# Three-layer graph kernel on one core: six pairs of gathered rows instead of four in the two attention walks, and the chain of segment maxima handed over in other pieces

## The chip, the cores and the metric

One core of one Trainium2 chip runs the whole program. The metric is the device time of one execution in microseconds (us), lower is better.

## The reference, cut to what matters

The program computes a graph-attention layer, a mixture of experts, a second graph layer and a routed feed-forward layer, all added to x. Only the attention layer is touched. It runs twice, first with 2 heads of 128 and then with 1 head of 256, over the same 100000 edges (sorted by destination) among 6250 nodes:

```python
z = (x @ W).reshape(num_nodes, heads, d)
el = jnp.einsum('nhd,hd->nh', z, a_l)
er = jnp.einsum('nhd,hd->nh', z, a_r)
e = el[src] + er[dst]
e = jnp.where(e > 0, e, NEG_SLOPE * e)
m = jax.ops.segment_max(e, dst, num_segments=num_nodes)
ex = jnp.exp(e - m[dst])
s = jax.ops.segment_sum(ex, dst, num_segments=num_nodes)
alpha = ex / s[dst]
msg = z[src] * alpha[:, :, None]
out = jax.ops.segment_sum(msg, dst, num_segments=num_nodes)
```

The second graph layer is a weighted mean over the same edges: it gathers in the same way and has no segment maxima.

## The kernel before

The phases follow one another: plan, rows1, walk1, walk2, post, dispatch, experts, combine, walk3, route, ffn. Walk1 and walk2 are `edge_walk` with two heads and with one head, walk3 is the weighted mean (another function, which the diff does not touch). In walk1 the node work of the layer between the two attentions rides along (`node`: a load of finished sums, a transpose, a product with the next weights, a store).

**Edges.** The sorted edges make 98 groups of 1024, each of 8 tiles of 128 edges (one edge per partition). One group is one step, two steps are one pair, so a walk has 98 steps, 49 pairs. The sums of a step go into a window of 80 nodes (`WIN`).

**What each engine does for a step or a pair.**

- GpSimd (POOL) gathers: `gather(s, k)` waits until the step that used the buffer before is done (`done8`) and until its indices stand in `idx[k]` (`idx_ready`), then issues 8 indirect DMAs (L583), one for each tile, 128 rows of z each. The rows go to `Z[k // 2]`; z carries el as an extra column.
- SyncE (SP) loads three small things for each pair (er of the window, two tables of resets): `load`, three pairs ahead (`AHEAD`).
- VectorE (DVE) finds the segment maxima of el (the chain, below), builds the one-hot tiles (`hot`, L803), looks up er for each edge (`targets`, L810 and L812), forms the logits (`logits`), scales (`hots`, L870 in walk1), and in walk1 divides the node sums (`node.scale`).
- ScalarE (ACT) takes the exponentials (`exps`, L610), scales rows or one-hot tiles by them (`scale`, 16 instructions per pair), and in `window` waits for the products of a step (`done8`), copies the next indices into `idx[k]` (`copy_idx`, L596), copies the window's sums out of PSUM (L633) and stores them.
- TensorE (PE) multiplies one-hot tiles by rows (`products`, L730, 8 matmuls per step in four quarters), and turns small things for the chain.

**The chain of maxima.** The maximum of e over a segment is taken from the maximum of el. For pair p: PE transposes the el column of the 16 tiles (`turn_el`, L693); DVE scans each tile from both sides (`scan_el`, L817 and L818; increments `ends_ready`); PE transposes the two end columns into one row (`turn_ends`, L699 and L700; `ends_turned`); DVE scans over the tiles (`carries`, L828 and L830, each head on its own; `ins_ready`); PE turns the carries back into columns (`turn_ins`, L705 and L706; `ins_turned`); DVE copies them (L837) and scans again with them (`scan_maxima`, L839 and L841; `max_ready`); PE transposes the result (`columns`, L711 and L712; `cols`); DVE forms the logits from it. That is three hand-overs DVE to PE and four PE to DVE for a pair, all in order. While PE multiplies pair p, both engines do the chain of pair p+2: `turn_el` behind quarter 0 of the first step, `turn_ends` behind quarter 2, `turn_ins` behind quarter 0 of the second step, `columns` at the end of the pair.

**Buffers.** `UNROLL = 8` steps are written out per turn of the loops, with one buffer each for indices and local targets and one `Z` for each two steps: four pairs of rows lie on chip, and the gathers of pair p+4 can start when pair p is done. Walk3 has eight step buffers too.

## Time and profile before

| | |
|---|---|
| three timed runs | 5286.85, 5288.94, 5299.87 us, median 5288.94 |
| profiled execution | 5308.62 us (span 5306.6), mean granted TensorE clock 0.749 |
| PE busy | 3058.9 us, 58% of the span |
| POOL busy | 2681.1 us, 51% |
| DVE busy | 1986.9 us, 37% |
| ACT busy | 1502.5 us, 28% |
| walk1 | from its first gather at 215 us to the end of its node work at 1571 us |
| walk2 | 1571 to 2805 us |
| walk3 | 3620 to 4870 us |

The span is that of one profiled execution, 19.7 us above the median of the timed runs. The busy shares are means over all phases: no engine is near 100%, and within a walk each engine waits for another one. What counts is therefore which wait ends last in each pair of steps.

### The profile page before, as it was taken

The page shows a single profiled execution, that of the slowest core. Times are in us where ns is not written, and L with a number is a line of the kernel's source. Part 1 is how long each engine was busy: PE and PEld are TensorE (multiplying, and loading weights), DVE is VectorE, ACT ScalarE, POOL GpSimd, SP SyncE. Part 2 cuts the span into 40 slices and gives each one's busy share as a digit, 9 for nine tenths or more (in the row PEclk, how much of TensorE's full clock was granted, in tenths as well). Part 3 has the DMA queues.
Part 4 walks back from the last instruction along what each step waited for, and adds up shares of the span by engine and source line. Part 5 has one row for each costly group of instructions (what it writes and reads, how often), then busy time and mean ns, then how long its engine had stood idle before and what let it go on. Part 6 is the DMA issues. An engine that isn't in the chain of part 4 may idle for free. (4 is left out here: it accounts for less than half of the span.)

```text
span 5306.6 us, 61698 instructions
## 1 busy us (share of the span) xinstructions
PE 3058.9 (58%) x11768; PEld 1883.0 (35%) x11768; DVE 1986.9 (37%) x5614; ACT 1502.5 (28%) x4807; POOL 2681.1 (51%) x2732
## 2 busy tenths in 40 slices
PE   3245555555543455554554489921566666666699
PEld 2123333332321222222223478820333333333466
DVE  4246555555533333333336812242222222223222
ACT  2122232332221222222221023311334444444233
POOL 1366666666626666666652145525566666661121
PEclk9667767777766767677775699965777777777799
DMA  6346666666623433333334266675444444442111
GB/s 151 82 97 104 107 106 109 107 108 104 104 52 96 98 95 99 97 97 98 95 90 135 64 200 220 225 226 153 108 123 120 122 119 122 120 122 65 63 55 51
DMA packets 381422, 598.24 MB, mean 113 GB/s; under 512 B 102442, under 2 KB 272078, under 8 KB 380658
## 3 DMA queue, kind: packets, MB, share of 16 engines
q0 software_dynamic: 136000, 386.29, 32.0%
q1 hardware_dynamic: 209138, 172.22, 12.0%
q10 hardware_dynamic: 36160, 38.56, 2.4%
q14 instruction: 104, 0.85, 0.1%
q8 instruction: 20, 0.33, 0.0%
HBM read 489.46 MB, written 107.34 MB: 112 GB/s over the span
## 5 line engine op out<-in xcount | busy, mean ns | idle before, releaser
L583 POOL DMA_INDIRECT walk_rows<-z_two_heads,walk_idx x784 | 794.7, 1014 | 536.3 <-ACT walk_idx L596 302.5
L583 POOL DMA_INDIRECT walk_rows<-z_one_head,walk_idx x784 | 758.3, 967 | 534.6 <-ACT walk_idx L596 301.9
L1861 POOL DMA_INDIRECT walk_rows<-h,walk_idx x784 | 747.5, 953 | 460.6 <-issue 232.8
L2006 PE MATMUL walk_ps_part<-walk_rows,walk_whot 128*80 128x257 f32 x1568 | 538.3, 479 | 244.1 <-issue 138.2
L730 PE MATMUL walk_ps_part<-walk_rows,walk_hot 128*80 128x258 f32 x1568 | 527.4, 469 | 0.6
L730 PE MATMUL walk_ps_part<-walk_rows,walk_whot 128*80 128x257 f32 x1568 | 519.0, 478 | 0.0
L2006 PEld LDWEIGHTS walk_ps_part<-walk_rows,walk_whot 128*80 128x80 f32 x1568 | 266.5, 186 | 441.4 <-issue 405.9
L596 ACT ACTIVATE walk_idx<-keep_src 128x8 int32 x212 | 44.1, 208 | 1293.5 <-remote 952.1
L730 PEld LDWEIGHTS walk_ps_part<-walk_rows,walk_whot 128*80 128x80 f32 x1568 | 267.9, 186 | 175.9 <-issue 127.1
L730 PEld LDWEIGHTS walk_ps_part<-walk_rows,walk_hot 128*80 128x80 f32 x1568 | 254.7, 180 | 132.2 <-issue 72.8
L812 DVE TENSOR_REDUCE walk_er<-walk_picked 128x8 f32<-128x640 f32 x294 | 241.0, 820 | 29.4 <-issue 7.6
L810 DVE TENSOR_TENSOR walk_picked<-walk_hot,walk_erB 128x640 f32<-128x640 f32 x294 | 241.0, 820 | 22.0 <-issue 3.1
L705 PE MATMUL walk_ps_row_scores<-walk_ones,walk_ends 1*32 1x1 f32 (+1 forms) x196 | 20.4, 171 | 384.2 <-DVEq L832 219.2
L624 ACT ACTIVATE walk_rows<-walk_rows,walk_w 128x129 f32<-128x129 f32 x784 | 235.3, 389 | 5.8
L699 PE MATMUL walk_ps_row_scores<-keep_ident,walk_fmax 32*1 32x32 f32 (+1 forms) x98 | 18.5, 188 | 369.6 <-issue 239.2
L1585 PE MATMUL exp_ps_hid<-exp_hT,exp_w 128*128 128x256 f32 x864 | 220.2, 388 | 8.3 <-DMA exp_b<-in_ffn_b 5.7
L1577 PE MATMUL exp_ps_y<-exp_w,exp_g 128*128 128x256 f32 x864 | 222.6, 380 | 0.0
L2120 DVE TENSOR_TENSOR walk_n_y<-walk_n_h,walk_ps_n_rows 128x256 f32<-128x256 f32 x52 | 21.9, 421 | 522.1 <-DMA walk_n_agg<-agg 459.0
L621 ACT ACTIVATE walk_whot<-walk_hot,walk_w 128x80 f32<-128x80 f32 x784 | 202.9, 347 | 20.5 <-issue 12.8
L1887 ACT ACTIVATE walk_whot<-walk_hot,walk_weight 128x80 f32<-128x80 f32 x784 | 206.8, 349 | 0.0
L828 DVE TENSOR_TENSOR_SCAN walk_ends<-walk_rr,walk_ends,walk_ps_row_scores 1x16 f32<-1x16 f32 x147 | 32.9, 224 | 453.1 <-remote 387.4
L1529 POOL DMA_INDIRECT y_tokens<-exp_y,exp_home x108 | 106.1, 982 | 183.1 <-DVE exp_y L1617 166.6
(368 smaller groups left out, 5189.3 us busy)
## 6 DMA issues: line engine op xcount, KB each, us to landing
exp_w<-in_ffn_W SPq DMA_DIRECT2D x108, 512.0 KB
agg<-walk_window ACTq DMA_DIRECT2D x198, 80.3 KB
walk_rows<-z_two_heads,walk_idx POOLq DMA_INDIRECT x784
walk_rows<-z_one_head,walk_idx POOLq DMA_INDIRECT x784
comb_ya<-y_tokens POOLq DMA_DIRECT2D x28, 448.0 KB
walk_rows<-h,walk_idx POOLq DMA_INDIRECT x784
walk_erB<-er_two_heads SPq DMA_DIRECT2D x104, 80.0 KB
agg<-walk_window ACTq DMA_DIRECT2D x99, 80.6 KB
```

What stands on the lines that cost most here:

```text
L583: pool.indirect_dma_start(out=Z[k // 2][:, k % 2 * GROUP_TILES + t, :], out_offset=None, in_=table, in_offset=bass.IndirectOffsetOnAxis(ap ...
L621: last = act.activation(S[k % HOTS][:, t, :], S0[k % HOTS][:, t, :], ACT.Copy, scale=w[:, 0, col:col + 1])
L624: last = act.activation(row, row, ACT.Copy, scale=w[:, 1, col:col + 1])
L730: last = pe.matmul(P[k % 2][0:WIN, 0:AW].rearrange("p (h w) -> p h w", w=HW), hot[:, t, :], rows, start=t == 0, stop=t == GROUP_TILES - 1)
L810: dve.tensor_tensor(picked[:, :, :], S0[k % HOTS][:, :, :], erB[q][:, j, :, h].unsqueeze(1).to_broadcast(wide), ALU.mult)
L812: dve.tensor_reduce(er[:, h, j * GROUP_TILES:(j + 1) * GROUP_TILES], picked[:, :, :], axis=AX.X, op=ALU.add)
L1529: pool.indirect_dma_start(out=dram["ys"], out_offset=bass.IndirectOffsetOnAxis(ap=home[k][:, t:t + 1], axis=0), in_=y[k][:, t, :], in_offs ...
L1577: last = pe.matmul(psY[k][t][:, 0:D], g[k][:, hc, t * 128:(t + 1) * 128], W2[k][:, hc, :], start=hc == 0, stop=hc == HC - 1)
L1585: last = pe.matmul(psH[hc % 2][:, 0:BLOCK], W1[k][:, hf, hc * 128:(hc + 1) * 128], hT[k][:, hf, :], start=hf == 0, stop=hf == HALVES - 1)
L1861: pool.indirect_dma_start(out=Z[k // 2][:, k % 2 * GROUP_TILES + t, :], out_offset=None, in_=table, in_offset=bass.IndirectOffsetOnAxis(ap ...
L1887: last = act.activation(S[k % HOTS][:, t, :], S0[k % HOTS][:, t, :], ACT.Copy, scale=weight[k][:, t:t + 1])
L2006: last = pe.matmul(P[k % 2][0:WIN, 0:HW], S[k % HOTS][:, t, :], Z[k // 2][:, k % 2 * GROUP_TILES + t, :], start=t == 0, stop=t == GROUP_TI ...
```

## The change

It changes `edge_walk` only (walk1 and walk2), the tables of `plan` that it reads, and nothing of walk3. Its parts:

1. **Depth.** In `edge_walk`, 12 steps are written out per turn in place of 8: six `Z` buffers in place of four, twelve `idx` and `dloc`, six of each of the small inputs, and 8 turns of the loop in place of 12. `AHEAD` goes from 3 to 5, `LOCAL_AHEAD` from 6 to 8. The plan computes the turns of these loops separately (five more small DVE instructions, two more numbers in a table).
2. **One hand-over of each kind for a pair.** `ends_ready`, `ends_turned`, `ins_ready` and `ins_turned` go; `el_scanned`, `rows_turned` and `rows_ready` come. PE's `turn_rows(r)` turns the end columns of pair r and the carries of pair r-1 together, with one increment of `rows_turned`; DVE's `scan_rows(r)` answers with the carries of pair r (`rows_ready`) and the maxima of pair r-1 (`max_ready`). A pair now has three hand-overs from DVE to PE and three from PE to DVE.
3. **Order.** While PE multiplies pair p it does `columns(p+1)` first, `turn_rows(p+3)` between the two steps, and `turn_el(p+4)` at the end. DVE does `weights(p+1)`, `scores(p+2)` (now only one-hot tiles and er, without a wait for PE), `node.scale(p+1)`, `scan_rows(p+3)`, `scan_el(p+4)`.
4. **Copies.** Since the transposed el must outlive its PSUM tile, `scan_el` copies it to `el_rows` (32x128 with two heads, 16x128 with one); `firsts` takes the place of `foremost` and the first of `ends`, with one more small copy; the el transpose has a PSUM bank of its own.
5. **Start.** Before its first product PE turns el of pairs 0 to 3, so it waits for the gathers of four pairs there; before, for those of two.

```diff
+EDGE_UNROLL = 12
+EDGE_LOOPS = (GROUPS - 2) // EDGE_UNROLL
...
-STEP_TAB = 2 * 96
+STEP_TAB = 2 * 104
...
+            dve.tensor_scalar(nie[:, :], ends[0:1, GROUPS - 1:GROUPS], float(GROUPS) + 0.5,
+                              float(EDGE_LONG - EDGE_LOOPS), ALU.is_gt, ALU.mult)
...
+    UNROLL = EDGE_UNROLL
...
-        LOCAL_AHEAD = 6
+        LOCAL_AHEAD = 8
...
-        AHEAD = 3
+        AHEAD = 5
...
-            def turn_ends(p):
-                pe.wait_ge(ends_ready, p + 1)
...
-            def turn_ins(p):
-                pe.wait_ge(ins_ready, p + 1)
...
+            def turn_rows(r, ends_too, ins_too):
+
+                if ends_too:
+                    pe.wait_ge(el_scanned, r + 1)
+                    pe.sem_inc(row_tick, 1)
+                if ins_too:
+                    pe.wait_ge(rows_ready, r)
+                    pe.sem_inc(row_tick, 1)
+                    pe.matmul(psK[:, 0:1], ends[:, 0:PT, :].rearrange("o t h -> o (t h)"), ones[:, 0:1], start=True, stop=True)
+                    last = pe.matmul(psK[:, 1:2], begins[:, 1:CT1, :].rearrange("o t h -> o (t h)"), ones[:, 0:1],
+                                     start=True, stop=True)
+                if ends_too:
+                    pe.transpose(psR[:, 0:ROWS], Fl[:, TILE - 1:TILE], ident[0:ROWS, 0:ROWS])
+                    last = pe.transpose(psR[:, ROWS:2 * ROWS], Bl[:, 0:1], ident[0:ROWS, 0:ROWS])
+                last.then_inc(rows_turned, 1)
...
+            def pair(p, m, s, turn, on):
+
+                if on(1):
+                    columns(p + 1, (m + 1) % 2)
                 products(s, 2 * m, 0)
-                if turn is not None:
-                    turn_el(p + 2, b, turn)
                 products(s, 2 * m, 1)
                 if node:
                     node.turn(pe, p, m % 2)
                 products(s, 2 * m, 2)
-                if turn is not None:
-                    turn_ends(p + 2)
                 products(s, 2 * m, 3)
                 if node:
                     node.products(pe, p, m % 2)
...
+                if on(2):
+                    turn_rows(p + 3, on(3), True)
+                for quarter in range(4):
                     products(s + 1, 2 * m + 1, quarter)
-                if turn is not None:
-                    columns(p + 2)
+                if on(4):
+                    turn_el(p + 4, (m + 4) % PAIRS, turn)
...
             for p in range(2):
                 turn_el(p, p, 1)
-                turn_ends(p)
-                turn_ins(p)
-                columns(p)
+                turn_rows(p, True, p > 0)
+            turn_el(2, 2, 1)
+            columns(0, 0)
+            turn_rows(2, True, True)
+            turn_el(3, 3, 1)
...
+            def scan_el(p, q, k, loaded):
+                dve.wait_ge(inputs[q], loaded)
                 dve.wait_ge(el_turned, p + 1)
...
+                dve.tensor_copy(el_rows[k][:, :], psT[:, :])
+                dve.drain().then_inc(el_scanned, 1)
+
+            def scan_rows(r, q, k, ends_too, ins_too):
+
+                dve.wait_ge(rows_turned, r + 1)
+                if ins_too:
+                    dve.tensor_copy(gkc[:, :], psK[:, :])
+                if ends_too:
...
+                    dve.tensor_copy(ends[:, 0, :], ends[:, PT, :])
+                    dve.drain()
...
+                    dve.drain()
+                    dve.tensor_tensor(firsts[k][:, 0, :], ends[:, 0, :], begins[:, 0, :], ALU.max)
+                    dve.tensor_copy(firsts[k][:, 1, :], ends[:, 0, :])
+                dve.drain().then_inc(rows_ready, 1)
...
                 weights(p + 1, m + 1, s + 2)
-                if turn is not None:
-                    scores(p + 2, m + 2, s + 4, turn)
+                if on(2):
+                    scores(m + 2, s + 4)
                 if node:
                     node.scale(dve, p + 1, (m + 1) % 2, half)
+                if on(2):
+                    scan_rows(p + 3, (m + 3) % INS, (m + 3) % 2, on(3), True)
+                if on(4):
+                    scan_el(p + 4, (m + 4) % INS, m % 2, loaded)
```

## Rows read from the trace of the kernel before

**Rows 1.** Windows of walk1, walk2, walk3: busy us (instructions) by engine, granted clock, DMA.

```profile
215.00:1571.00 1356.00, 727.75 (x2762) 404.61 (x2762) 732.79 (x1779) 380.00 (x1397) 794.67 (x784) 0.71 0.58 100
1571.00:2805.00 1234.00, 609.90 (x2254) 315.25 (x2254) 401.20 (x1133) 291.12 (x1141) 758.31 (x784) 0.71 0.38 95
3620.00:4870.00 1250.00, 767.95 (x2636) 429.82 (x2636) 290.16 (x965) 502.02 (x1623) 747.51 (x784) 0.74 0.43 115
```

**Rows 2.** Page, costliest groups: the gathers of the three walks.

```profile
L583 POOL DMA_INDIRECT walk_rows<-z_two_heads,walk_idx x784 | 794.7, 1014 | 536.3 <-ACT walk_idx L596 302.5
L583 POOL DMA_INDIRECT walk_rows<-z_one_head,walk_idx x784 | 758.3, 967 | 534.6 <-ACT walk_idx L596 301.9
L1861 POOL DMA_INDIRECT walk_rows<-h,walk_idx x784 | 747.5, 953 | 460.6 <-issue 232.8
```

**Rows 3.** Waits of POOL, 300:1478, 1667:2742, 3761:4783: us, times, longest.

```profile
POOL walk_rows L583 <- ACT walk_idx L596: 232.6, 54, 16.0
...
POOL walk_rows L583 <- ACT walk_idx L596: 198.0, 48, 11.7
...
POOL walk_rows L1861 <- ACT walk_idx L1874: 176.7, 43, 4.8
```

**Rows 4.** Source lines of the window copies: ns min/median/max, first and last start.

```profile
L633 ACT ACTIVATE walk_window<-walk_ps_part x90: 362/364/383, 313.0 to 1461.1; 80x258 f32<-80x258 f32 x90
L633 ACT ACTIVATE walk_window<-walk_ps_part x7: 363/364/382, 1477.8 to 1526.8; 80x258 f32<-80x258 f32 x7
...
L633 ACT ACTIVATE walk_window<-walk_ps_part x89: 362/364/383, 1666.6 to 2742.1; 80x257 f32<-80x257 f32 x89
```

**Rows 5.** Timeline of POOL: end of the first burst and restart, walk1 and walk2.

```profile
215.08 1.04 POOL L583 DMA_INDIRECT walk_rows<-z_two_heads,walk_idx  x1 [69.64 <-ACT walk_idx L596]
...
297.03 0.95 POOL L583 DMA_INDIRECT walk_rows<-z_two_heads,walk_idx  x1 [0.30 <-issue]
313.93 1.15 POOL L583 DMA_INDIRECT walk_rows<-z_two_heads,walk_idx  x1 [15.95 <-ACT walk_idx L596]
...
1667.51 0.97 POOL L583 DMA_INDIRECT walk_rows<-z_one_head,walk_idx  x1 [11.66 <-ACT walk_idx L596]
```

**Rows 6.** Timeline of POOL, PE, DVE and ACT around one burst of walk2.

```profile
2085.85 0.95 POOL L583 DMA_INDIRECT walk_rows<-z_one_head,walk_idx  x1 [4.50 <-ACT walk_idx L596]
...
2104.71 0.95 POOL L583 DMA_INDIRECT walk_rows<-z_one_head,walk_idx  x1 [0.30 <-issue]
...
2093.69 1.53 PE L730 MATMUL walk_ps_part<-walk_rows,walk_whot 128*80 128x257 f32 x6
2105.08 0.19 PE L705 MATMUL walk_ps_row_scores<-walk_ones,walk_ends 1*16 1x1 f32 x2 [9.87 <-issue]
...
2108.98 0.21 ACT L596 ACTIVATE walk_idx<-keep_src 128x8 int32 x1 [14.51 <-remote]
...
2104.59 0.23 DVE L828 TENSOR_TENSOR_SCAN walk_ends<-walk_rr,walk_ends,walk_ps_row_scores 1x16 f32<-1x16 f32 x1 [11.19 <-remote]
```

**Rows 7.** Waits of all engines in walk1, 400 to 1400 us.

```profile
DVE walk_gkc L837 <- remote: 209.3, 15, 17.1
...
PEld walk_ps_cols L711 <- DVEq L843: 186.2, 17, 14.0
```

**Rows 8.** Timeline of ACT, window copies at the end of walk2 (seven).

```profile
2774.38 0.36 ACT L633 ACTIVATE walk_window<-walk_ps_part 80x257 f32<-80x257 f32 x1
...
2801.77 0.36 ACT L633 ACTIVATE walk_window<-walk_ps_part 80x257 f32<-80x257 f32 x1
```

**Rows 9.** Timeline of PE in the first burst of walk3.

```profile
3688.88 1.02 PE L2005 MATMUL walk_ps_part<-walk_window,walk_carry 80*1 80x257 f32 x2 [36.36 <-issue]
```

**Rows 10.** Groups by line, DVE in walk1, 500 to 1400 us.

```profile
L817 DVE TENSOR_TENSOR_SCAN walk_fmax<-walk_reset,walk_ps_row_scores 32x128 f32<-32x128 f32 x35 | 14.1, 402 | 10.9 <-remote 9.3 <-issue 1.6
...
L837 DVE COPY walk_gkc<-walk_ps_row_scores 32x2 f32<-32x2 f32 x35 | 5.2, 147 | 212.9 <-remote 181.5 <-issue 26.2 <-PE walk_ps_row_scores L706 4.3
```

**Rows 11.** Source line L583 in walk1: ns min/median/max, first and last start.

```profile
L583 POOL DMA_INDIRECT walk_rows<-z_two_heads,walk_idx x784: 947/953/1630, 215.1 to 1475.4; - x196
```

More of the change, by code:

```diff
@@ L479, in edge_walk @@
         M = ph.sb("smax", [ROWS, TILE])
-        row_ends = ph.sb("ends", [1, 1 + CT1, H])
-        foremost, ends = row_ends[:, 0, :], row_ends[:, 1:CT1 + 1, :]
+        ends = ph.sb("ends", [1, CT1, H])
+        firsts = [ph.sb(f"firsts{k}", [1, 2, H]) for k in range(2)]
+        el_rows = [ph.sb(f"el_rows{k}", [ROWS, TILE]) for k in range(2)]
         begins = ph.sb("begins", [1, CT1, H])
@@ L532, in load @@
             def load(p, q):
[L533 removed]
+                sp.wait_ge(inputs_used6, p + 1)
                 sp.sem_inc(sp_tick, 1)
@@ L819, in scan_el @@
                                        ALU.add, ALU.max)
-                dve.tensor_copy(ends[:, 0, :], ends[:, PT, :])
-                dve.drain().then_inc(ends_ready, 1)
-            def carries(p, q):
-                dve.wait_ge(ends_turned, p + 1)
-                turned = psR[:, :].rearrange("o (c t h) -> o c h t", c=2, h=H)
-                reset = rr[q][:, :, :, :, :].rearrange("o c h j t -> o c h (j t)")
-                for h in range(H):
-                    dve.tensor_tensor_scan(ends[:, 1:CT1, h], reset[:, 0, h, :], turned[:, 0, h, :],
-                                           ends[:, 0, h:h + 1], ALU.add, ALU.max)
-                    dve.tensor_tensor_scan(begins[:, PT - 1::-1, h], reset[:, 1, h, ::-1], turned[:, 1, h, ::-1],
-                                           -BIG, ALU.add, ALU.max)
-                dve.drain().then_inc(ins_ready, 1)
-                dve.tensor_tensor(foremost, ends[:, 0, :], begins[:, 0, :], ALU.max)
@@ new lines, in scan_el @@
+                dve.drain().then_inc(el_scanned, 1)
[4 more added lines that the diff above has]
+                if ends_too:
+                    turned = psR[:, :].rearrange("o (c t h) -> o c h t", c=2, h=H)
+                    reset = rr[q][:, :, :, :, :].rearrange("o c h j t -> o c h (j t)")
+                    dve.tensor_copy(ends[:, 0, :], ends[:, PT, :])
+                    dve.drain()
+                    for h in range(H):
+                        dve.tensor_tensor_scan(ends[:, 1:CT1, h], reset[:, 0, h, :], turned[:, 0, h, :],
+                                               ends[:, 0, h:h + 1], ALU.add, ALU.max)
+                        dve.tensor_tensor_scan(begins[:, PT - 1::-1, h], reset[:, 1, h, ::-1], turned[:, 1, h, ::-1],
+                                               -BIG, ALU.add, ALU.max)
+                    dve.drain()
+                    dve.tensor_tensor(firsts[k][:, 0, :], ends[:, 0, :], begins[:, 0, :], ALU.max)
+                    dve.tensor_copy(firsts[k][:, 1, :], ends[:, 0, :])
+                dve.drain().then_inc(rows_ready, 1)
+                if ins_too:
+                    before = (q + INS - 1) % INS
+                    dve.tensor_tensor_scan(Cf, R[before][:, 0:TILE], el_rows[1 - k][:, :], gkc[:, 0:1], ALU.add, ALU.max)
+                    dve.drain()
+                    dve.tensor_tensor_scan(M[:, TILE - 1::-1], R[before][:, TILE:0:-1], Cf[:, TILE - 1::-1], gkc[:, 1:2],
+                                           ALU.add, ALU.max)
+                    dve.drain().then_inc(max_ready, 1)
@@ L871, in hots, with scores @@
                 last.then_inc(hot_ready, 1)
-            def scores(p, m, s, loaded):
-                q = m % INS
-                dve.wait_ge(inputs[q], loaded)
-                scan_el(p, q)
+            def scores(m, s):
                 hot(s, 2 * m % UNROLL)
                 hot(s + 1, (2 * m + 1) % UNROLL)
-                carries(p, q)
-                targets(q, 0, 2 * m % UNROLL)
-                scan_maxima(p, q)
-                targets(q, 1, (2 * m + 1) % UNROLL)
+                dve.drain()
+                for j in range(2):
+                    targets(m % INS, j, (2 * m + j) % UNROLL)
             def weights(p, m, s):
@@ L890, in weights, with pair @@
                 hots(s + 1, (2 * m + 1) % UNROLL, W[m % 2])
-            def pair(p, m, s, half, turn):
+            def pair(p, m, s, half, loaded, on):
                 weights(p + 1, m + 1, s + 2)
-                if turn is not None:
-                    scores(p + 2, m + 2, s + 4, turn)
+                if on(2):
+                    scores(m + 2, s + 4)
                 if node:
                     node.scale(dve, p + 1, (m + 1) % 2, half)
+                if on(2):
+                    scan_rows(p + 3, (m + 3) % INS, (m + 3) % 2, on(3), True)
+                if on(4):
+                    scan_el(p + 4, (m + 4) % INS, m % 2, loaded)
             n, rest = turns(dve), rest_of(dve)
-            scores(0, 0, 0, LOADS)
+            for p in range(2):
+                scan_el(p, p, p % 2, LOADS)
+                scan_rows(p, p, p % 2, True, p > 0)
+            scan_el(2, 2, 0, LOADS)
+            scores(0, 0)
             weights(0, 0, 0)
-            scores(1, 1, 2, LOADS)
+            scan_rows(2, 2, 0, True, True)
+            scores(1, 2)
+            scan_el(3, 3, 1, LOADS)
             if node:
```

73 lines of the change are left out of this document (27 added, 46 removed).

## The prediction, made before the changed kernel ran

> **What bounds the kernel now.** I read the windows by stage first. In none of the three walks is an engine full: POOL, the busiest, has 795, 758 and 748 us of 1356, 1234 and 1250, and the DMA engines are at 0.58, 0.38 and 0.43 [rows 1]. Then the costliest groups: the gathers are the same 784 in each walk, and what releases them after idle time is the ACT copy of the next indices [rows 2]. That copy waits for the products of the step that held the buffer, so POOL waits for the consumers.
>
> A gather takes 1014, 967 or 953 ns [rows 2] and 0.30 us of issue follows it [rows 5], so the 16 of a pair cost 16 x 1.314 = 21.0 us in walk1, 16 x 1.267 = 20.3 in walk2, 16 x 1.253 = 20.0 in walk3. The waits for a released buffer, without the first one, are (232.6 - 16.0)/45 = 4.8 us per pair in walk1, (198.0 - 11.7)/44 = 4.2 in walk2, and 176.7/43 = 4.1 each in walk3 [rows 3]. The sums are 25.8, 24.5 and 24.1 us per pair. The window copies give the same: 313.0 to 1477.8 us for 90 steps is 25.9 per pair, 1666.6 to 2742.1 for 88 steps is 24.4 [rows 4].
>
> The reader is to see two things. First, walk3, which has no chain of maxima at all, is only 0.3 us per pair faster than walk2. Second, the shape of a period in the timeline: 16 gathers start from 2085.85 to 2104.71. PE finished a step at about 2095.2 (1.53 us of L730 from 2093.69), yet ACT saw it at 2108.98; DVE went on with L828 at 2104.59 after 11.19 us, and PE with L705 at 2105.08 after 9.87 [rows 6]. So hand-overs made in the second half of a burst of gathers are seen about when it ends, and POOL's gap of 4 us is what lies between the burst's end and the release that was late. The first burst of walk3 shows the same without any chain: PE idle for 36.36 us in it [rows 9]. I call this the hold. I don't know its cause, only its shape.
>
> Walk1's extra against walk2 is 25.9 - 24.4 = 1.5 us per pair. Half of it is the gather itself (0.7), the rest gaps: 53 waits for 45 pairs, where walk2 has 47 for 44 [rows 3]. Here the chain shows: PE's weight load at `columns` waits 186.2 us for DVE's L843 in 1000 us, DVE 209.3 us at L837 [rows 7].
>
> **The change, part by part.**
>
> *Start.* 96 gathers fit before POOL waits, where 64 did. 32 more at 1.256 us (0.95 + 0.30 [rows 5]) are 40.2 us. In walk1 the first release came 313.0 - 215.1 = 97.9 us after the first gather [rows 4, 5], 80.4 of it the burst; PE now waits for four pairs there and is held besides. I put all 40.2 us on the path, in each walk. The lower bound is 0, if step 0 were done within the burst; walk3's first is, but that burst held PE for 36 us [rows 9].
>
> *End.* After the last gather six pairs are on chip in place of four. Without gathers a pair takes (1526.8 - 1477.8)/3.5 = 14.0 us in walk1 (eight copies, of which the profile holds seven [rows 4]) and (2801.77 - 2774.38)/3 = 9.1 in walk2 [rows 8]. So two pairs of the steady part move to this pace: 43 steady pairs stay in walk1 (of 45) and 42 in walk2 (of 44).
>
> *Hand-overs.* One of four from PE to DVE goes, and the three left stand a pair or two ahead of their use; `turn_el(p)` waits for rows released two pairs before, no longer one. A late hand-over delays the chain only if it is more than about half a pair late. Bounds of walk1's period: below, that of walk3, 24.1, above, today's 25.9. If every extra gap goes and the slower gathers stay, it is 21.0 + 4.2 = 25.2; if the slower gathers go too, 24.4. I take the middle, 24.8. In walk2 the bounds are 24.1 and 24.4, and I take 24.3.
>
> *DVE's added work.* The copy of el to `el_rows` is at most a scan of the same tile (402 ns, L817) and at least L837's 147 ns; the second copy to `firsts` is one like L837 [rows 10], and there are two drains more. Together 0.3 to 0.9 us per pair. DVE is busy 733 of 1356 us in walk1, 15.0 us per pair [rows 1], so its cover is the 25.9 - 15.0 = 10.9 us per pair in which it waits. Without it, it would cost 0.9 x 49 = 44 us in walk1. I take nothing.
>
> *Moved:* `turn_rows`, `columns` and `turn_el` issue the same six kinds of small PE matmuls as before. No DMA and no queue of POOL or SP is moved; SP's loads run five pairs ahead in place of three, 6 small loads more at the start, under the 120 us burst. Behind DVE's new wait at `scan_rows` stand `scan_el(p+4)` and `weights(p+2)`, for which ACT's exponentials and then PE's next products wait; it hangs on PE's half pair. *Plan:* five small DVE instructions and a drain, at 0.15 to 0.2 us, about 1 us, uncovered. *Loops:* 8 turns for 12, nothing.
>
> *A rule against it.* Walk1's gathers have a median of 953 ns but reach 1630 [rows 11], a mean of 1014 [rows 2], so something lengthens some of them. The Trainium skill ("SBUF — State Buffer", "A bandwidth-pool intuition that's wrong") says that an fp32 copy from SBUF to SBUF on DVE locks GpSimd out of writing its descriptors, so that DMAs from its queue starve. The trace agrees in kind only: it does not show which DVE instruction stood beside a long gather. By that rule the added SBUF copy would lengthen gathers, and the time would be rival E's below; by the rows alone, which price the copy at 147 ns beside idle time, it adds nothing.
>
> **The sum**, against the profiled execution of 5308.6 us:
> Walk1: 40.2 + 43 x 24.8 + 2 x 14.0 - 1164.8 = -30.2.
> Walk2: 40.2 + 42 x 24.3 + 2 x 9.1 - 1075.5 = +3.5.
> Plan: +1. Together -25.7, so 5282.9 us profiled. The profiled execution stood 19.7 us above the median of the runs shown; the forecast as a median is 5263 us.
>
> **The rivals.**
>
> *B, longer bursts pay.* With six pairs on chip and a looser chain the consumers may release two pairs between waits, and the gap of 4.2 us comes once in two pairs: 21.0 + 2.1 = 23.1 in walk1, 20.3 + 2.1 = 22.4 in walk2. For it: walk2's first 64 gathers with their gap of 11.66 us [rows 5] come to (64 x 1.267 + 11.4)/64 = 1.44 us per gather, 23.1 per pair. Against it: the consumers stand still in a long burst and have to catch up after it, and POOL restarts at the first released step, however many buffers there are. Sum: walk1 -103, walk2 -76, so 5110 us. At its far end POOL never waits (21.0 and 20.3 per pair): -194 and -165, so 4931 us.
>
> *D, only the gaps go.* Walk1 at 25.2, walk2 at 24.4 as before: 68.2 + 43 x 25.2 - 1164.8 = -13, walk2 58.4 + 42 x 24.4 - 1075.5 = +8, plan +1: 5285 us, no change.
>
> *C, the other side: the longer first burst is paid and the pace stays.* If the hold and not the chain sets walk1's 25.9, the fewer hand-overs are hidden anyway and both walks lose their start: 68.2 + 43 x 25.9 - 1164.8 = +17, walk2 +8, plan +1: 5315 us; and if the consumers catch up slowly, so that the end gives nothing back, up to 5289 + 2 x 40.2 = 5369. For it: walk2 and walk3 have the same period with and without a chain. Against it: walk1's waits at L711 and L837, which walk3 has not. It decides from a walk1 period of about 25.8 on.
>
> *E, longer gathers.* If the added work lengthens one gather of each pair from 953 to 1630 ns [rows 11], that is 0.68 x 98 = 66 us on the forecast: 5329. Against it: walk1's DVE does nearly twice walk2's work [rows 1] and its gathers are only 47 ns longer in the mean [rows 2]. The Trainium skill's rule above is what would make this one.
>
> **How the numbers follow.** 0.3% (16 us) is what a measurement of this kernel can tell from no change. Chances: my forecast 0.40, B 0.14 and its far end 0.03, D 0.21, C 0.19, E 0.03. The forecast's own range goes from 24.4 to 25.1 us per pair in walk1 and reaches half the start's cost up, 5240 to 5295; 0.06 of its 0.40 lies within 0.3% of no change. So faster is 0.34 + 0.17 = 0.51, same 0.21 + 0.06 = 0.27, slower 0.19 + 0.03 = 0.22. The range takes in B, E and most of C: 5105 to 5335; outside are B's far end, C's upper part and some of B, under 0.2 together.
>
> **What the profile after would show.** The first wait of POOL in each walk after 96 gathers, some 40 us later than now. In between, waits of about 4 us, 45 or fewer per walk; B would show half as many. The waits at `columns` behind the second scan's drain and at the copy of the carries should all but vanish in walk1 if the chain mattered; walk3 should not move. Gathers should keep their means of 1014 and 967 ns; longer ones would speak for the skill's rule. The forecast is wrong if the gaps stay at 4.8 us per pair in walk1 (C), or if POOL's wait falls below 3 us per pair (B).

## The result, and the profile after

The changed kernel takes 5351.1 us (median of 4 runs, 5348.1 to 5389.5), the kernel before 5290.5 (5286.9 to 5299.9): a ratio of 1.0117, 95% interval 1.0089 to 1.0145. It is slower by some 60 us, where 26 us of gain were forecast. The profiled execution of after has a span of 5346.4 us, 39.8 above that of before. The profile of before stood 18 us above its median and that of after 3 us below its own, so 21 of the 60 us stand in no stretch of the two profiles.

Page of after, costliest groups: the gathers, to be held against [rows 2].

```profile
L595 POOL DMA_INDIRECT walk_rows<-z_two_heads,walk_idx x784 | 808.3, 1031 | 502.0 <-ACT walk_idx L608 264.0
L595 POOL DMA_INDIRECT walk_rows<-z_one_head,walk_idx x784 | 771.8, 984 | 550.2 <-ACT walk_idx L608 322.3
L1885 POOL DMA_INDIRECT walk_rows<-h,walk_idx x784 | 749.4, 956 | 468.7 <-issue 235.8
```

Source lines of the window copies in after (ns min/median/max, first and last start): the first 85 steps of walk1, its last 13, the first 85 of walk2, and its last 14, of which the first is the 85th again.

```profile
L645 ACT ACTIVATE walk_window<-walk_ps_part x85: 363/365/383, 356.3 to 1428.1; 80x258 f32<-80x258 f32 x85
...
L645 ACT ACTIVATE walk_window<-walk_ps_part x13: 363/370/383, 1440.9 to 1552.3; 80x258 f32<-80x258 f32 x13
...
L645 ACT ACTIVATE walk_window<-walk_ps_part x85: 361/365/384, 1723.1 to 2752.8; 80x257 f32<-80x257 f32 x85
...
L645 ACT ACTIVATE walk_window<-walk_ps_part x14: 363/364/372, 2752.8 to 2829.3; 80x257 f32<-80x257 f32 x14
```

The same lines of before, for the same steps:

```profile
L633 ACT ACTIVATE walk_window<-walk_ps_part x85: 362/364/383, 313.0 to 1401.7; 80x258 f32<-80x258 f32 x85
...
L633 ACT ACTIVATE walk_window<-walk_ps_part x14: 362/364/382, 1401.7 to 1530.2; 80x258 f32<-80x258 f32 x14
...
L633 ACT ACTIVATE walk_window<-walk_ps_part x85: 362/364/383, 1666.6 to 2697.5; 80x257 f32<-80x257 f32 x85
```

Timeline of POOL in after: first gather of walk1, the restart after 96 gathers.

```profile
220.57 1.03 POOL L595 DMA_INDIRECT walk_rows<-z_two_heads,walk_idx  x1 [79.06 <-ACT walk_idx L608]
...
343.27 0.95 POOL L595 DMA_INDIRECT walk_rows<-z_two_heads,walk_idx  x1 [0.30 <-issue]
357.18 1.41 POOL L595 DMA_INDIRECT walk_rows<-z_two_heads,walk_idx  x1 [12.96 <-ACT walk_idx L608]
```

The reader can take the 39.8 us of the two spans apart with these:

| stretch | before | after | difference |
|---|---|---|---|
| first gather of walk1 | 215.1 | 220.6 | +5.5 |
| walk1: first gather to first window copy | 97.9 | 135.7 | +37.8 |
| walk1: 42 pairs (84 steps) | 1088.7, 25.92 per pair | 1071.8, 25.52 per pair | -16.9 |
| walk1: from there to the last copy | 128.5 | 124.2 | -4.3 |
| to the first gather of walk2 | 44.6 | 40.2 | -4.4 |
| walk2: first gather to first window copy | 91.8 | 130.6 | +38.8 |
| walk2: 42 pairs | 1030.9, 24.55 per pair | 1029.7, 24.52 per pair | -1.2 |
| walk2: from there to the last copy | 104.3 | 76.5 | -27.8 |
| all behind it (walk3 +10.0, unchanged code) | 2504.8 | 2517.1 | +12.3 |

So the first window copy comes as much later as was forecast, in both walks. What was to pay for it, walk1's pace, is little better, and walk1 gives nearly nothing back at its end.

The prediction said that the two waits of [rows 7] would all but vanish in walk1 if the chain mattered. One did. In walk1 of after, from 400 to 1400 us, DVE at the copy of the carries, and PE's weight load at `columns`:

```profile
DVE walk_gkc L840 <- remote: 3.2, 1, 3.2
...
PEld walk_ps_cols L726 <- issue: 107.8, 25, 9.9
PEld walk_ps_cols L726 <- DVEq L861: 55.0, 14, 12.5
```

DVE's was 209.3 us and is gone. PE's at `columns` is 163 us in two rows, 108 of it without a releaser that the profile shows, where it was 194 (186.2, and 8.2 without one). And PE now waits at the product of the node work too, for the Relu of ACT that makes its input. Before and after, in the same window:

```profile
PEld walk_ps_n_z L411 <- ACT walk_n_hT L385: 25.1, 6, 6.6
```

```profile
PEld walk_ps_n_z L421 <- ACT walk_n_hT L395: 166.9, 21, 15.1
```

### The profile page after: what moved, and what is told of

Same layout as the page of the kernel before. It is cut to its first block and busy times, and to the rows that moved or that the text cites. A ratio compares the mean times of both kernels' runs of the same rounds, so it can differ in the third digit from the quotient of the medians.

```text
span 5346.4 us, 62209 instructions
## 1 busy us (share of the span) xinstructions
PE 3052.7 (57%) x11768; PEld 1912.8 (36%) x11768; DVE 2027.2 (38%) x5813; ACT 1508.1 (28%) x4819; POOL 2711.4 (51%) x2732
## 5 line engine op out<-in xcount | busy, mean ns | idle before, releaser
L595 POOL DMA_INDIRECT walk_rows<-z_two_heads,walk_idx x784 | 808.3, 1031 | 502.0 <-ACT walk_idx L608 264.0
L595 POOL DMA_INDIRECT walk_rows<-z_one_head,walk_idx x784 | 771.8, 984 | 550.2 <-ACT walk_idx L608 322.3
L2030 PE MATMUL walk_ps_part<-walk_rows,walk_whot 128*80 128x257 f32 x1568 | 530.7, 474 | 219.3 <-issue 125.7
L745 PE MATMUL walk_ps_part<-walk_rows,walk_hot 128*80 128x258 f32 x1568 | 513.9, 479 | 3.4 <-issue 3.4
L745 PE MATMUL walk_ps_part<-walk_rows,walk_whot 128*80 128x257 f32 x1568 | 505.6, 478 | 4.8 <-issue 4.8
L742 PE MATMUL walk_ps_part<-walk_window,walk_carry 80*1 80x129 f32 (+1 forms) x588 | 137.1, 345 | 491.6 <-ACT walk_window L645 478.6
L745 PEld LDWEIGHTS walk_ps_part<-walk_rows,walk_hot 128*80 128x80 f32 x1568 | 276.8, 189 | 157.1 <-issue 105.9
L421 PE MATMUL walk_ps_n_z<-walk_n_w,walk_n_hT 128*128 128x258 f32 x208 | 98.7, 623 | 311.6 <-ACT walk_n_hT L395 174.9
L742 PEld LDWEIGHTS walk_ps_part<-walk_window,walk_carry 80*1 80x1 f32 x588 | 33.6, 82 | 576.8 <-ACT walk_window L645 503.9
```

Source lines behind the costliest of these rows:

```text
L595: pool.indirect_dma_start(out=Z[k // 2][:, k % 2 * GROUP_TILES + t, :], out_offset=None, in_=table, in_offset=bass.IndirectOffsetOnAxis(ap ...
L742: pe.matmul(P[k % 2][0:1, cols], CE[k % HOTS][:, h:h + 1], wsb[1 - k % 2][:, cols], start=False, stop=False)
L745: last = pe.matmul(P[k % 2][0:WIN, 0:AW].rearrange("p (h w) -> p h w", w=HW), hot[:, t, :], rows, start=t == 0, stop=t == GROUP_TILES - 1)
L2030: last = pe.matmul(P[k % 2][0:WIN, 0:HW], S[k % HOTS][:, t, :], Z[k // 2][:, k % 2 * GROUP_TILES + t, :], start=t == 0, stop=t == GROUP_TI ...
```

## Two regimes

The first experiments went to another chip, and it showed something that no profile before had: POOL never waited for long for a released buffer. Every walk was one burst of 784 gathers, and the same kernel before took 4667 us in place of 5290. I had not expected this. The waits of POOL in the kernel before there (run e12, from 230 to 1300 us), against [rows 3]:

```profile
POOL walk_rows L583 <- issue: 222.5, 730, 0.3
POOL walk_rows L583 <- ACT walk_idx L596: 9.4, 31, 0.3
```

and its gathers and last window copies of walk1, beside those of the changed kernel on the same chip (run e13):

```profile
L583 POOL DMA_INDIRECT walk_rows<-z_two_heads,walk_idx x784: 949/953/1602, 216.5 to 1284.2; - x196
...
L633 ACT ACTIVATE walk_window<-walk_ps_part x7: 363/364/383, 1284.6 to 1332.7; 80x258 f32<-80x258 f32 x7
```

```profile
L595 POOL DMA_INDIRECT walk_rows<-z_two_heads,walk_idx x784: 949/953/1597, 231.9 to 1295.7; - x196
...
L645 ACT ACTIVATE walk_window<-walk_ps_part x9: 363/371/383, 1298.4 to 1363.0; 80x258 f32<-80x258 f32 x9
```

I call the regime of the first profiles the waiting one (the first measurement, e5 to e7, e16 to e18) and this one the free one (e1 to e4, e8 to e15). Each of the groups e1 to e4, e5 to e7, e8 to e11, e12 to e15 and e16 to e18 ran on one chip, the first and the third group on the same one, and each ratio is against the kernel before on that chip in that group. In the free regime the hand-overs are not held up in a burst (the first window copy of e12 comes 72 us after its first gather, while POOL gathers on for 1068 us; in before it came after 98 us, behind the burst of 64), a gather costs what it cost in the waiting one (953 ns in the median), and the gathers alone set the pace: 1.36 us each in walk1, 20.5 us per pair in walk2. What makes a chip show the one or the other stays open. The granted clock in walk1 is 0.71 in before and 0.74 in e12, so nearly the same.

## The experiments

**e1, depth alone.** The old chain, with twelve steps written out:

```diff
+    UNROLL = EDGE_UNROLL
...
-        AHEAD = 3
+        AHEAD = 5
```

(with the tables of the plan).

> The chain of maxima as before, but twelve steps and six pairs of rows on chip, loads five pairs ahead, and the plan's table as in the change. Theory S (the first burst of gathers is paid and the pace stays with the hold): both walks start some 40 us later than before and their pace is 25.9 and 24.5 us per pair as before; about +10 us in walk2, +17 to +25 in walk1, so the whole kernel is as slow as the changed one, 5340 to 5360 us. Rival K (the new chain costs what the depth would have gained): without the new chain depth shows its worth, walk1 below 25 us per pair and the kernel at or under 5290 us. Rival P (the plan and its table cost several us): the first gather of walk1 comes at 220 us, not 215.

Free regime: 4685.5 us against 4666.7, 1.0041 (1.0028 to 1.0055). The sign of rival P is there, a first gather at 225.5 us, but its cause is not: e8 and e9 below put it down to the loads of SP, and with the weights first the first gather of the changed kernel, with the longer plan, comes no later than that of the kernel before (180.4 and 182.0 us). Neither S nor K was tested.

**e2, depth alone, held to four pairs.**

```diff
-                pool.wait_ge(done8, s + 1)
+                pool.wait_ge(done8, s + 5)
```

> As the run with depth alone, but POOL waits for four steps more before each gather, so that only four pairs are ever on chip: what is left of the change is the loops' form, the loads further ahead and the plan's table. Theory S: the time of the kernel before, 5285 to 5300 us, plus at most the few us of a later first gather; the first gap comes after 64 gathers. Rival L (the longer loop bodies or the plan cost the time): as slow as the changed kernel, 5340 us or more.

1.0041 (1.0026 to 1.0057), the same as e1. In the free regime depth is worth nothing and costs nothing; its surroundings cost some 20 us, 13 of them ahead of the first gather (229.3 us, against 216.5 in e12, the kernel before on another free chip). Neither expectation was tested.

**e3, the changed kernel held to five pairs** (`s + 3` in that wait).

> The changed kernel, but POOL waits for two steps more before each gather: five pairs on chip, the first burst 80 gathers. Theory S: each walk's first release comes 20 us earlier than in the changed kernel, the pace stays within 0.3 us per pair, and walk2's end takes one pair less at the fast pace (-20 + 15): in all 10 to 25 us faster than the changed kernel, 5325 to 5340 us. Rival K2 (the new chain needs the depth): turn_el waits for rows, walk1 and walk2 go to 26 us per pair or more, and the kernel is slower than the changed one.

1.0105 (1.0081 to 1.0129); free regime, where POOL had nothing to wait for, so it told nothing of the first burst (e17 does).

**e4, the first burst split.**

```diff
...
+            for j in range(UNROLL):
+                gather(j + 2, (j + 2) % UNROLL, max(j + 3, UNROLL + 1 if j + 2 >= 8 else 0))
...
-            with pool.Fori(0, n) as i:
+            with pool.Fori(0, rest_of(pool)) as i:
...
```

> The changed kernel, but in the first turn the gathers of steps 8 to 11 wait until step 0 is done, so that the first burst is 64 gathers and the depth is filled up later. Theory S1 (the consumers stand still for as long as POOL gathers, so 32 gathers more cost 40 us wherever they stand): the first window copy comes 38 us earlier, but the burst behind it is 32 gathers or more longer, and from step 20 on all is as in the changed kernel: 5340 to 5360 us. Rival S2 (only the first release counts): the walks keep the 38 us and the kernel comes to 5280 us or less.

1.0153 (1.0129 to 1.0176). In the free regime the two pauses of 13 and 11 us that it adds to a POOL that never waits are simply paid: against e3, which never waits there either, 4740.4 - 4717.8 = 22.6 us. Neither theory was tested.

**e5, the kernel before.**

> The kernel before, unchanged, for its profile beside the others of this call. In the four runs so far POOL never waited for a released buffer: all 784 gathers of a walk were one burst of 1.27 to 1.36 us each. Theory F (there are two regimes, and in the free one the gathers alone set a walk's pace): this kernel shows the same, a pace of 20.5 us per pair in walk2, and its first gather of walk1 some 5 us before the 225 to 229 us seen in those. Rival: with the buffers of before, POOL waits here as it did in the first profile, 24.5 us per pair.

Waiting regime, 5310.5 us. The rival held: the same kernel took 4667 us beside e1 to e4, and on each chip all kernels showed one regime, so it goes with the chip, not with the kernel.

**e6, the changed kernel.**

> The changed kernel, unchanged, beside the others of this call. Theory F: where the gathers alone set the pace, more depth changes nothing in it, and the change costs only its start and its end: PE's first product waits for the rows of pair 3 (two pairs later) and every product stays two pairs further behind the gathers, so that at the end of walk1 and walk2 two pairs more are left when the last gather is out. With 16 to 17 us per pair in walk1 and 9 to 13 in walk2 that is about 45 us, and 5 us more from the plan: a ratio of 1.010 to 1.012. Rival (depth helps or hurts beyond that): a pace in walk2 more than 0.3 us per pair off the 20.5 of the kernel before.

1.0101 (1.0063 to 1.0139), the first result again. First gather at 229.6 us, 12.7 later than e5. The chip was a waiting one, so theory F was not tested here (e13 does).

**e7, one wait of the new chain in the old one.** To e1 was added:

```diff
+                if late is not None:
+                    rows_landed((m + 4) % PAIRS, late)
```

`rows_landed` waits for the two steps of gathers of pair p+4, at the end of pair p; PE also waits so for pairs 2 and 3 before its first product.

> The old chain with six pairs on chip, and one thing of the new one: at the end of pair p PE also waits until the rows of pair p+4 have landed, and at the start for those of pairs 2 and 3. Nothing else is added. Theory F (the wait for rows two pairs further ahead is the whole cost): this is as slow as the run of the changed kernel, within 10 us, so 20 to 30 us slower than the old chain with six pairs (which was at 1.0041 of the kernel before, this at 1.009 to 1.012). Rival C (the new chain's copies, drains and order cost the time): within 5 us of the old chain's 1.0041.

Waiting regime: 1.0147 (1.0101 to 1.0194). The median is 19.5 us above that of the changed kernel (e6), but the intervals overlap, and they overlap with that of the same kernel without the wait (e16, on another chip) too. So in this regime the run decides nothing on the wait.

**e8 and e9, node weights first**, in the changed kernel and in the kernel before:

```diff
+            if node:
+                node.start_sp(sp)
             for p in range(AHEAD + 1):
                 load(p, p % INS)
             if node:
-                node.start_sp(sp)
                 node.load(sp, 0, 0, row_of(sp, 0), None, None)
```

> The changed kernel, but SP issues walk1's four loads of node weights ahead of the loads of the first pairs, where both kernels have them behind. Theory Q (walk1's first gather waits, by way of ACT's and DVE's start, for the last of those weights, and SP's 12 loads of steps at 3.5 us each stand ahead of them, 8 in the kernel before): the first gather comes at about 187 to 192 us, not at 220 to 230, and the whole kernel is 30 to 40 us faster than the changed one, which puts it at a ratio of 1.002 to 1.005 to the kernel before. Rival: the first gather stays where it was, since something else holds it.

> The kernel before with the same one edit: node weights ahead of the loads of the first pairs. Theory Q: the first gather at 187 to 192 us where it was at 215 to 217, and the kernel 22 to 28 us faster than before, a ratio of 0.995 to 0.996. Rival: the gain is lost, because the loads of the first pairs now come later and the first scans wait for them; then within 5 us of the kernel before.

Free regime: the changed kernel goes to 1.0012 (1.0002 to 1.0021), from 1.0116 (e13), the kernel before to 0.992 (0.9904 to 0.9937). Between the two, with this edit in both, 39 us remain (4675.1 - 4636.1). Both gain more than expected. First gathers at 180.4 and 182.0 us. SP's queue in after (first load of a step, last weight), then in e9:

```profile
172.22 0.39 SPq L550 DMA_DIRECT2D walk_erB<-er_two_heads  x1
...
215.58 0.43 SPq L362 DMA_DIRECT2D walk_n_bcol<-in_b_gat  x1
```

```profile
175.18 0.41 SPq L349 DMA_DIRECT2D walk_n_w<-in_W  x1
...
176.62 0.43 SPq L352 DMA_DIRECT2D walk_n_bcol<-in_b_gat  x1
178.63 0.35 SPq L538 DMA_DIRECT2D walk_erB<-er_two_heads  x1
```

In after the weights stand 43 us behind the first load, and ACT's first index copy waits for them:

```profile
219.42 0.21 ACT L608 ACTIVATE walk_idx<-keep_src 128x8 int32 x1 [59.49 <-DMA walk_n_bcol<-in_b_gat]
```

**e10, e11: e1 and e3 again.**

> Once more the old chain with six pairs on chip; it has been run only on a chip where POOL never waited. If POOL waits here for released buffers as in the first profiles: theory S says that the first release of each walk comes 38 to 44 us later than before and walk1's pace is 25.6 to 25.9 us per pair as before, while the new chain has 25.2 to 25.5; the kernel at a ratio of 1.010 to 1.013. The rival, that depth alone brings the pace down, has walk1 at 25.3 or below. If POOL never waits here: 1.004 as before.

> Once more the changed kernel held to five pairs on chip. If POOL waits for released buffers here: theory S says that both walks release first 20 us earlier than the changed kernel, keep its pace within 0.3 us per pair, and give 9 to 16 us less back at the end of each; 10 to 20 us faster than the changed kernel, a ratio of 1.006 to 1.009. Rival K2 (the new chain needs all six): a pace above 26 in walk1 or 25 in walk2, and slower than the changed kernel. If POOL never waits here: 1.0105 as before.

Free regime both: 1.0042 (1.0027 to 1.0056) and 1.0096 (1.0079 to 1.0113), as the first time.

**e12 to e15, four kernels on one chip.**

> The kernel before, unchanged, for a profile on the chip of this call. Where POOL never waits for a released buffer: first gather of walk1 at 215 to 217 us, one burst of 784 gathers in each walk, 20.5 us per pair in walk2, the last gather of walk1 some 45 to 50 us ahead of its last window copy. Where POOL waits: as in the first profile.

> The changed kernel, unchanged, on the chip of this call. Where POOL never waits: theory F, 0 us from the pace, 13 us from SP's longer start, and 30 to 35 us because PE waits for rows two pairs further ahead (later first product, 20 to 25 us more left at the end of walk1 and 11 at the end of walk2): a ratio of 1.009 to 1.012 and no difference to the same kernel held to five pairs. Where POOL waits: 1.010 to 1.012 as before, and 38 to 44 us from the first burst in each walk.

> The old chain with six pairs and PE's wait for the rows of pair p+4 at the end of pair p. It was slower than the changed kernel where POOL waits (1.0147). Where POOL never waits, theory F gives it the changed kernel's time within 10 us: 1.008 to 1.012. Rival C (the new chain's own work costs the time): 1.004 to 1.005, as the old chain with six pairs without that wait.

> The kernel before with the node weights ahead of the loads of the first pairs. Where POOL never waits: a ratio of 0.992 as before, the first gather at 182 us. Where POOL waits: the same 33 us at the start, and nothing given back, since the pace does not hang on it: 5311 - 33, a ratio of 0.994. Rival: where POOL waits, the start is taken back by later waits and the ratio is 0.998 or more.

Free regime. e13, the changed kernel: 1.0116 (1.0099 to 1.0133). e14, the old chain with the one wait: 1.0101 (1.0080 to 1.0123), where it is 1.0041 and 1.0042 without it (e1, e10). So that wait alone costs some 28 us in this regime. The new chain's own work (rival C of this run) is left with at most the 0.0015 between e13 and e14, 7 us, which their intervals don't tell from nothing. e15: 0.9941 (0.9919 to 0.9963).

The spans of e12 and e13 (4669.4 and 4717.7 us) differ by 48.3: first gather 216.5 to 231.9, +15.4; walk1 from first gather to last copy 1116.2 to 1131.1, +14.9, in which the gathers end 3.9 us sooner and the last copy comes 18.8 us later behind them; walk2 1035.5 to 1049.0, +13.5, of which 10.2 behind the last gather; all else +4.5. PE's waits from 350 to 1250 us in e12 and e3 show who is late in this regime, the rows themselves:

```profile
PE walk_ps_row_scores L693 <- DMA walk_rows<-z_two_heads,walk_idx: 363.7, 41, 10.9
```

```profile
PE walk_ps_el L705 <- DMA walk_rows<-z_two_heads,walk_idx: 255.5, 34, 12.1
```

`turn_el` waits there for rows of pair p+4 in place of p+2, before products whose rows landed long ago.

**e16 to e18, the waiting regime.**

> The old chain with six pairs on chip, sent again for a chip on which POOL waits for released buffers. There: theory S, the first burst is 96 gathers and the first release 38 to 44 us later in each walk, walk1's pace 25.6 to 25.9 us per pair (the new chain: 25.2 to 25.5), the ratio 1.008 to 1.012. Rival: depth alone brings walk1 to 25.3 or below and the ratio is 1.006 or less. Where POOL never waits: 1.004 again.

> The changed kernel held to five pairs on chip, sent again for a chip on which POOL waits. There: theory S, first release in each walk 20 us earlier than in the changed kernel, 10 to 17 us less given back at the end, pace as in the changed kernel: a ratio of 1.007 to 1.010 against its 1.010 to 1.012. Rival K2: turn_el comes to wait for rows, pace above 26 us in walk1, ratio above 1.012. Where POOL never waits: 1.010 again.

> The kernel before with the node weights ahead of the loads of the first pairs, sent again for a chip on which POOL waits. There: first gather at 182 to 187 us, 30 us ahead of before, and the kernel 30 us faster, a ratio of 0.993 to 0.996; the rival, that later waits take it back, has 0.998 or more. Where POOL never waits: 0.992 to 0.994 again.

e16, depth alone: 1.0125 (1.0100 to 1.0151), the start as theory S has it and the kernel a little slower; its rival is out. e17, the new chain on five pairs: 0.9983 (0.9971 to 0.9996), which neither theory had: S wanted 1.007 to 1.010, and it misjudged what the sixth pair costs. e18: 0.9956 (0.9936 to 0.9976), as expected. The window copies of the first 85 steps: e16 walk1 and walk2, e17 walk1 and walk2, e18 walk1.

```profile
L644 ACT ACTIVATE walk_window<-walk_ps_part x85: 362/364/383, 355.8 to 1462.3; 80x258 f32<-80x258 f32 x85
...
L644 ACT ACTIVATE walk_window<-walk_ps_part x85: 362/364/382, 1737.1 to 2787.6; 80x257 f32<-80x257 f32 x85
```

```profile
L645 ACT ACTIVATE walk_window<-walk_ps_part x85: 362/365/383, 347.9 to 1408.5; 80x258 f32<-80x258 f32 x85
...
L645 ACT ACTIVATE walk_window<-walk_ps_part x85: 363/364/383, 1700.4 to 2702.1; 80x257 f32<-80x257 f32 x85
```

```profile
L634 ACT ACTIVATE walk_window<-walk_ps_part x85: 363/365/383, 291.6 to 1367.0; 80x258 f32<-80x258 f32 x85
```

All profiles of the waiting regime: from the first gather to the first and to the 13th window copy, the pace of the 42 pairs behind the first copy and of the 36 behind the 13th, and the whole from first gather to last copy, walk1 / walk2:

| kernel | first copy | 13th copy | pace of 42 | pace of 36 | whole |
|---|---|---|---|---|---|
| old chain, 4 pairs (before; e5; e18) | 98, 98, 107 / 92, 92, 91 | 254, 250, 260 / 240, 240, 239 | 25.9, 25.6, 25.6 / 24.5, 24.3, 24.5 | 25.9, 25.6, 25.6 / 24.5, 24.2, 24.5 | 1315, 1315, 1317 / 1227, 1223, 1225 |
| old chain, 6 pairs (e16) | 126 / 113 | 293 / 282 | 26.3 / 25.0 | 26.1 / 24.5 | 1346 / 1243 |
| the same with the late wait (e7) | 131 / 117 | 291 / 281 | 26.1 / 25.1 | 26.0 / 24.7 | 1337 / 1246 |
| new chain, 6 pairs (after; e6) | 136, 136 / 131, 136 | 284, 286 / 280, 282 | 25.5, 25.2 / 24.5, 24.4 | 25.6, 25.2 / 24.4, 24.4 | 1332, 1312 / 1237, 1236 |
| new chain, 5 pairs (e17) | 120 / 122 | 265 / 260 | 25.3 / 23.9 | 25.4 / 24.0 | 1307 / 1213 |

The two paces differ because the first six pairs belong to the start. In walk2 of e16 ACT copied the first indices at 1736.97 us, inside POOL's burst (1623.9 to 1755.3), and the next ones only at 1772.64, behind it:

```profile
1736.97 0.21 ACT L607 ACTIVATE walk_idx<-keep_src 128x8 int32 x1 [41.79 <-remote]
...
1772.64 0.21 ACT L607 ACTIVATE walk_idx<-keep_src 128x8 int32 x1 [33.64 <-remote]
```

So the first copy is too early a mark for the cost of the burst, and a pace counted from it holds a part of that cost. From the 13th copy to the 85th, walk2 takes the same time with four pairs (e18) and with six (e16):

```profile
L634 ACT ACTIVATE walk_window<-walk_ps_part x73: 363/365/383, 1785.9 to 2668.1; 80x257 f32<-80x257 f32 x73
```

```profile
L644 ACT ACTIVATE walk_window<-walk_ps_part x73: 362/364/382, 1905.6 to 2787.6; 80x257 f32<-80x257 f32 x73
```

## Why the prediction was wrong

The time, 5351, lies above the range (5105 to 5335), and the sign was wrong. What came is nearest to rival C (0.19): the longer first burst is paid and the pace stays, or nearly. With the measured paces, 25.5 and 24.5, the forecast's own sum gives +13 us in place of -26; the two profiles are 39.8 apart, and of the other 27 us 20 are walk1's end and 12 lie behind walk2, with 5 the other way. Step by step:

- *Start, right in the waiting regime.* 40.2 us on the path in each walk were counted. The first copy comes 37.8 and 38.8 us later; at the 13th copy it is 31 and 41 us (before and after), 36 and 41 (e5 and e6). Held to five pairs (e17) the 13th copy comes 21 and 22 us sooner than in e6, for 20 us of gathers. Depth alone does it too: 43 us in walk2 and 33 in walk1 (e16 against e18). In the free regime, where no buffer is waited for, the first copy is 25 and 23 us later all the same (e12 and e13), which is PE's wait for four pairs at the start (the old chain with that wait, e14, has 93 and 91 us to the first copy, without it, e1, 73 and 69).
- *Pace of walk1, the step that failed.* The forecast said: "I take the middle, 24.8." Measured are 25.5 and 25.2, against 25.9 and 25.6: 0.4 us per pair and 17 us in all, where 46 were counted (behind the 13th copy 0.3 and 0.4). The bound of 24.4 took walk1's extra gaps for waits of the chain that would go with it. DVE's wait at the carries did go, and the gaps of POOL nearly stayed: PE's wait at `columns` is 163 us where it was 194, and in front of the node product it waits for ACT 166.9 us where it waited 25.1 (e6: 162 and 168.3; e5: 167 and 14.5). PE's idle time moved more than it shrank. Depth alone (e16) lowered DVE's wait to 109.6 us and PE's at `columns` to 93, at a pace no better than before, so these waits are not what holds POOL. What does set walk1's pace, the node product or the hold, no run here takes apart. POOL's waits in after are 184.6 us in 45 from 356 us on, so (184.6 - 13.0)/43 = 4.0 us per pair where they were 4.8: neither C's 4.8 nor B's 3. The gathers grew by 17 ns, 0.3 us per pair, and 25.9 - 0.8 + 0.3 is 25.4, about what is seen.
- *Depth is a cost at the start and buys no pace.* With the chain left alone, two pairs more make the kernel 1.0125 of before (e16). Against e18 they make walk1 and walk2 29 and 18 us longer: in walk2 43 us at the start and 24 given back at the end, at the same pace of 24.5; in walk1 33 at the start, 21 given back, and 16 from a pace of 26.1 against 25.6, which is little beyond what before, e5 and e18 differ by (25.6 to 25.9). With the new chain, six pairs are at 1.0101 and 1.0117 and five at 0.9983, each against the kernel before on its own chip, so the sixth pair costs over 1%, the first burst included; that five pairs run walk2 at 24.0 where all others have 24.2 to 24.7 is not explained. That the chain helps is not clear of noise: its pace in walk1 is 0.3 to 0.4 us per pair lower in two pairs of profiles, but the intervals of e16 (1.0100 to 1.0151), e6 (1.0063 to 1.0139) and the first result (1.0089 to 1.0145) overlap. The old chain on five pairs was not run.
- *End.* Walk2 gave back 27.8 us near what was computed (two pairs from 24.5 to 9.1 are 30.8). Walk1 gave back 4.3 in the first profile and 24.3 in e6. The 14.0 us per pair came from a misread row: the eighth copy of [rows 4] was not lost but fell at 1530.2, outside the window that I had read, so the pace is (1530.2 - 1477.8)/3.5 = 15.0; that is 2 us of the sum. Why the two profiles of the changed kernel differ by 20 us at this place stays open.
- *SP's queue, the second step that failed.* The forecast had "6 small loads more at the start, under the 120 us burst". They are 12 (three for each of the four added steps), 3.5 us of SP for each step, and stand not beside the burst but ahead of it: SP issues them before the node weights, for which ACT's first index copy waits, for which POOL waits. The view of before held it, POOL's 69.64 us in front of 215.08 [rows 5]. The four steps are 14 us in every profile. The first gather is 12.7 us later in e6 than in e5 and 15.4 in e13 than in e12; in the first pair of profiles it is only 5.5, because SP's first load came 8.3 us sooner in after (172.2 against 180.55 us). e8 and e9 show the mechanism. With the weights first the first gather of the kernel before comes 31 to 35 us sooner as well, and that kernel is 33, 26 and 19 us faster (medians of e9, e15, e18); in e18 the first window copy gave 9 us back, 107 us behind the first gather in place of 98.
- *The wait two pairs further ahead.* I counted it as slack. In the free regime it is the larger part of the loss (e14; 28 of some 54 us): the consumers stay two pairs further behind the gathers, and what is left at the last gather is paid without cover. In the waiting regime no run shows its worth (e7).
- *Longer gathers (rival E).* The means rose by 17 ns in both walks, 13 us each in the profile of after, but in the free regime they are 1059 and 1054 ns in walk1 (e12, e13) and 976 and 980 in walk2, so there the added copies do not lengthen them. In the waiting regime walk1's means are 1009 to 1017 ns in the five profiles with the old chain and 1021 to 1036 in the three with the new one, so a few ns each can't be excluded; walk2's overlap. The rule that the prediction takes from the Trainium skill ("SBUF — State Buffer", "A bandwidth-pool intuition that's wrong"), for copies from SBUF to SBUF, is hardly tested here: those that the change adds hold one or two numbers, and the copy of el comes from PSUM.
- *Walk3*, whose code is the same, took 1249 to 1250 us in after, e6 and e16 and 1237 to 1246 in the others of the waiting regime. That part of the 39.8 us, up to 10 us, stays open.

The best version run is the kernel before with the weights first: 0.992 and 0.9941 in the free regime, 0.9956 in the waiting one. The new chain on five pairs with the weights first was not run.

## What to carry to other kernels

Follow the wait ahead of the first transfer through every queue before you call anything issued at the start hidden: a prefetch depth is also that many more instructions ahead of whatever stands behind them. When consumers set the pace, one more buffer only lengthens the first burst, and the end gives back less than that; try one buffer less as well as one more. Read a pace from where the start has died away, not from the first release. A wait that goes is worth nothing until another engine's gap closes with it: look where the idle time went. And measure on more than one chip before you explain a pace by waits.

## What the runs showed of the hardware

- The same program takes 4666 to 4669 us on some chips and 5290 to 5311 on others. On the first POOL issues 784 gathers of a walk without a wait longer than 0.3 us for a buffer (e12, walk1); on the second it waits some 4 us for each pair, and in the burst of [rows 6] its release came only behind the last of 16 gathers. That is no strict rule: in e16 one release came inside the first burst of walk2. Untouched walk3 takes 990 us in the one (e12) and 1239 to 1246 in the other (before, e5), with gathers of 949 and 953 ns in the mean.
- In the waiting regime each pair of gathers more in the first burst put walk2's 13th window copy 20 to 22 us later (239 to 240 us with four pairs, 260 with five, 280 to 282 with six), and the pace behind it did not hang on the depth (24.5 in e18 and e16).
- Packets of the instruction queue rise from 104 to 196 with the longer loops; in the free regime e1 and e2 are 19 and 20 us slower than before, 9 and 13 of it ahead of the first gather, so at most 8 to 10 us can be theirs, as an estimate. That was not tested by itself.
